# A layer of decayed linear attention and a looked-up gated network: queries and keys made in seven block products for eight, and four operations of the down stage issued earlier

## The reference

```
q = xn Wq;  k_i = xn Wk[i];  v_i = xn Wv[i]        (i = 0, 1, 2; each 512 -> 128)
gate = softmax(xn Wg)                              (3 per row)
blended = sum_i gate_i * ((q k_i^T * w_i) v_i)     (w_i: causal decay, strictly after)
s = blended Wo * out_scale                         (128 -> 512)
h = silu(xn Wgate^T) * (xn Wup^T)                  (512 -> 1376)
out = x + s * silu(h Wdown^T)                      (1376 -> 512)
```

## Time and profile before

| | |
|---|---|
| time, median of 3 runs | 1836.87 us (1836.4 to 1838.73) |
| the profiled execution's own time | 1841.18 us |
| its span in the trace | 1839.1 us |
| PE busy | 97% of the span |
| PE weight loads busy | 77% |
| DVE, POOL, ACT busy | 71%, 56%, 44% |
| mean granted clock of PE | 0.998 |

### The profile page before, as it was taken

How to read it: one execution, slowest core, us unless ns; L and a number is a source line. 1 busy time by engine, 2 the same in 40 slices (tenths; PEclk the granted TensorE clock), 3 DMA queues, 4 the chain that set the end, 5 groups by cost and what they waited for, 6 DMA issues and landing times.

```text
span 1839.1 us, 41728 instructions
## 1 busy us (share of the span) xinstructions
PE 1792.9 (97%) x15944; PEld 1419.5 (77%) x15944; DVE 1302.6 (71%) x2629; ACT 812.7 (44%) x1406; POOL 1026.8 (56%) x1041
## 2 busy tenths in 40 slices
PE   5899999999999999999999999999999999999997
PEld 2337879788787978788787978878796887879786
DVE  6885858686776867677685767768585867758574
ACT  3784444444444443444444444444444444444433
POOL 9303736556473746547374665647375564737363
PEclk9999999999999999999999999999999999999999
DMA  9986685958678676967768696876859686786753
GB/s 219 329 305 175 168 232 162 254 160 228 192 191 219 169 230 165 255 170 196 211 178 221 168 249 163 224 201 173 228 168 237 165 236 181 184 223 168 209 149 112
DMA packets 411028, 370.90 MB, mean 202 GB/s; under 512 B 222577, under 2 KB 278641, under 8 KB 410753
## 3 DMA queue, kind: packets, MB, share of 16 engines
q1 hardware_dynamic: 399824, 361.36, 71.0%
q0 software_dynamic: 11008, 6.89, 2.5%
HBM read 294.34 MB, written 35.52 MB: 179 GB/s over the span
## 4 chain that ended last, share of the span: by engine, by line
PE 90%; DMA 5%; ACT 1%; POOL 1%; issue 1%; DVE 1%; SPq 0%; POOLq 0%; ACTq 0%; DVEq 0%
PE F L1870 44%; PE F L1909 17%; PE B L1750 16%; DMA region<-mixed_half 3%; PE B L1782 2%; PE F L1890 2%; PE B L1757 2%; PE B L1755 2%; PE B L1756 2%; PE F L1657 1%; POOL codes L728 1%; PE F L1755 1%; PE F L1756 1%; PE F L1757 1%; DMA dblocks<-xt 1%
## 5 line engine op out<-in xcount | busy, mean ns | idle before, releaser
L1870 PE MATMUL F<-xtc,ring 128*128 128x256 f16 (+1 forms) x4224 | 497.7, 273 | 0.0
L1870 PEld LDWEIGHTS F<-xtc,ring 128*128 128x128 f16 (+1 forms) x4224 | 416.0, 100 | 42.4
L1909 PE MATMUL F<-ring,region 128*128 128x256 f16 x3360 | 382.5, 273 | 0.0
L1870 PE MATMUL F<-xt,ring 128*128 128x256 f16 (+1 forms) x3168 | 377.2, 273 | 0.0
L1909 PEld LDWEIGHTS F<-ring,region 128*128 128x128 f16 x3360 | 328.0, 98 | 47.9
L1870 PEld LDWEIGHTS F<-xt,ring 128*128 128x128 f16 (+1 forms) x3168 | 310.8, 100 | 33.3
L923 ACT ACTIVATE region<-region 128x512 f16<-128x512 f32 (+3 forms) x256 | 130.3, 509 | 270.8 <-DVE region L1531 115.7
L832 POOL TENSOR_TENSOR region<-hs,region 128x1024 f16<-128x1024 f32 x80 | 175.4, 2192 | 104.1 <-ACT region L923 104.1
L850 POOL TENSOR_TENSOR x_out<-x_out,region 128x512 f32<-128x512 f32 x64 | 81.0, 1266 | 133.7 <-DVE region L1602 133.7
L923 ACT ACTIVATE region<-F 128x512 f32<-128x512 f32 (+2 forms) x168 | 95.9, 573 | 129.6 <-PE F L1909 84.2
L1750 PE MATMUL B<-xt,a_hi 128*128 128x512 f16 x512 | 152.3, 379 | 0.0
(11 more groups left out here) (269 smaller groups left out, 3361.4 us busy)
## 6 DMA issues: line engine op xcount, KB each, us to landing
ring<-blocks SPq DMA_DIRECT2D x546, 256.0 KB, 3.3
ring<-dblocks SPq DMA_DIRECT2D x224, 256.0 KB, 3.5
x_next<-in_x SPq DMA_DIRECT2D x64, 256.0 KB, 4.3
x_out<-in_x SPq DMA_DIRECT2D x64, 256.0 KB, 3.2
out_y<-x_out SPq DMA_DIRECT2D x64, 256.0 KB, 4.9
ring<-blocks SPq DMA_DIRECT2D x112, 128.0 KB, 2.5
ring<-dblocks SPq DMA_DIRECT2D x112, 128.0 KB, 3.1
blocks<-ring SPq DMA_DIRECT2D x35, 256.0 KB, 7.6
```

Of the source, the lines that this page charges most:

```text
L1870: ins = T_.matmul(out_, a, b, start=fresh, stop=False, skip_group_check=True)
L1909: ins = T_.matmul(bank[:, j * HV:(j + 1) * HV], a, b, start=fresh, stop=False, skip_group_check=True)
```

## The change

**Seven products for eight.** Queries and keys become a set of their own, QK = -1, ahead of the six. `queries_keys` now calls the same `product` as the sets. The 512 x 512 matrix [Wq Wk0 Wk1 Wk2], scaled, is the operand in blocks; S1, S2 and S3 are held in the new tensor `qsum`, S4 in place of a block of `a_hi` and `a_lo` that no product uses alone. A product is 2 x 2 x 3 = 12 matmuls of 256 columns, into the banks F0 to F3 in place of B0 and B1. ACT and DVE run `first_copy`, `u2`, `u4`, `c22`, `c12` and `c21` for it, and take the halves of q and the keys from the four result blocks (`qk_high`, `qk_low`) in place of four banks.

**Build.** DVE scales Wq and Wk in place and makes the four sums and their low halves; ACT takes the four high halves, two after step 33 and two after step 34. `plus`, `minus`, the pick matrices, `eye` and `ht` move to other memory.

**Order.** SP issues `blend(3)` after slot 8, ahead of the load of `x_next`, and `turn_sums(1)` after slot 12. ACT issues `x_sums_high(1)` ahead of `partial(2)` in place of after `attn_out(1)`, POOL `x_sums_low(1)` ahead of `finish(0)` in place of after it. Semaphore s_pp counts 49 products a group for 42.

```diff
+    QK = -1
+    SPG = NSET + 1
+    QSUM = {S1: 0, S2: 1, S3: 2}
+    QBASE = {A11: (0, 0), A12: (2, 0), A22: (2, 2 * P), S4: (0, 2 * P)}
...
+        QKB = ((ZC, 2, HALF), (FB[0].rearrange("p (m t) -> p m t", m=2), 0, 0), (YC, 0, HALF), (XC[0], 2, 0))
...
+        QSUM_AT = {NU: (0, 1), NU + 1: (2, 3)}
...
+                    if m == 8:
+                        blend(3)
                     if m == 8 and ahead:
                         sp.wait_ge(s_xh, gi * GT + 2 * GT)
                         sp.sem_inc(s_go, 1)
                         load_x(row_group(i + 1, g))
-                    if m == 10:
-                        blend(3)
-                    if m == 13 and not last:
+                    if m == 12 and not last:
                         turn_sums(1)
...
                     x_sums(1)
+                    x_sums_low(1)
                 finish(0)
-                if not last:
-                    x_sums_low(1)
                 finish(1)
...
+                if b in QSUM_AT:
+                    for n in QSUM_AT[b]:
+                        act.wait_ge(s_scale, 2 + n + 1)
+                        copy(qs_half(n, 0), sums[n]).then_inc(s_ahi, 1)
...
+                def qk_high(n):
+
+                    done = ((s_c22, of_set(gi, QK) + 1), (s_pp, made(gi, QK, 4)), (s_c12, of_set(gi, QK) + 1),
+                            (s_c21, of_set(gi, QK) + 1))[n]
+                    block, j0, t0 = QKB[n]
+                    act.wait_ge(*done)
+                    if n == 0:
+                        act.wait_ge(s_y1, gi * GT + GT)
+                    if j0 == 0:
+                        copy(q32[:, t0:t0 + HALF], block[:, 0], scale=2.0 ** QP).then_inc(s_q32, 1)
+                    copy(qk_hi[:, j0:j0 + 2, t0:t0 + HALF], block, scale=2.0 ** QP).then_inc(s_qk, 1)
+
+                first_copy(QK)
+                if not last:
+                    act.wait_ge(s_dwr[ND - 1], 16)
+                    x_high(0, gi * GT + GT + 1)
+                    x_high(1, gi * GT + GT + 2)
+                for n in range(4):
+                    qk_high(n)
...
                 attn_out(0)
+                if not last:
+                    x_sums_high(1)
                 partial(2)
                 attn_out(1)
-                if not last:
-                    x_sums_high(1)
...
+            def product(i, g, s, p):
+
...
+                if p == 0:
+                    bank, k0, cols = FB[0], 0, lo
+                    pe.wait_ge(*((s_z, gi * GT + FREE) if s == QK else (s_qkl, gi * 4 + 2) if s == 0 else
+                                 (s_sg1, gi * NSET + s)))
+                elif p == 1:
+                    bank, c = FB[1], T2
+                    pe.wait_ge(*((s_g, gi * GT + FREE) if s == QK else (s_u2, prev)))
+                    if s == QK:
+                        pe.wait_ge(s_xtc, 32 * (gi + FREE))
+                        pe.wait_ge(s_alo, len(MATS) + 4)
+                elif p == 2:
+                    bank, c = FB[3], T1
+                    pe.wait_ge(*((s_ca, gi * GT + FREE) if s == QK else (s_c12, prev)))
...
             def queries_keys(i, g):
                 gi = i * GPB + g
-                xh, xl = xt_hi[:, g], xt_lo[:, g]
-
                 for t in range(GT):
                     pe.wait_ge(s_xt[t], 16 * (gi + FREE))
-                for j in range(1 + NH):
...
-                    three(B[j % 2], [(a_hi[:, k, j * D:(j + 1) * D], a_lo[:, k, j * D:(j + 1) * D],
-                                      xh[:, k], xl[:, k]) for k in range(KC)], GRP).then_inc(s_pqk, 1)
+                for p in range(NP):
+                    product(i, g, QK, p)
```

More of the change, by code:

```diff
@@ L234, in attention_ffn_kernel @@
         mixed_half = sb("mixed_half", [P, 2, 2, D], F16)
-        plus = sb("plus", [P, P], F16)
-        minus = sb("minus", [P, P], F16)
+        qsum = sb("qsum", [P, 3, 2, BANK], F16)
         mask = sb("mask", [P, NH, P], F32)
         flip = mixed
+        plus, minus = mixed_half[:, 0, 0], mixed_half[:, 0, 1]
+        pick_hi, pick_lo = (mixed_half[:, 1, n].rearrange("p (q r) -> p q r", q=CG) for n in range(2))
+        eye = hs[:, 3, 0:QR]
+        lutpick = hs[:, 3, QR:QR + CG * CG].rearrange("p (q c) -> p q c", q=CG)
         fade_row = faded[:, :].rearrange("p (h t) -> p h t", h=NH)
@@ L313, in attention_ffn_kernel @@
             pos += n
+        fb = ctx.enter_context(nc.psum_tensor("F", [P, 4, BANK], F32))
+        FB = [fb[:, n] for n in range(4)]
         def halves(k, **dims):
@@ L339, in attention_ffn_kernel, with qs_half @@
         wo32 = q32
+        qs32 = [xp[:, n] for n in range(2)] + [hs[:, 2 * n:2 * n + 2].rearrange("p a t -> p (a t)") for n in range(2)]
+        sums = [v.rearrange("p (k c) -> p k c", k=2) for v in qs32]
+        def qs_half(n, lo):
+            if n < 3:
+                return qsum[:, n, lo].rearrange("p (k c) -> p k c", k=2)
+            return (a_hi, a_lo)[lo][:, 0:2, 2 * P:4 * P]
         staged = region[:, n_oh + KC * QKV:n_oh + KC * QKV + 4 * BANK * 2].bitcast(F16).rearrange(
@@ L516, in attention_ffn_kernel, with shape, of_set, made @@
         FREE = 1
+        def shape(s):
+            return (P, 2) if s == QK else (FM[MS[s][0]], len(MS[s]))
+        def of_set(gi, s):
+            return gi * SPG + s + 1
+        def made(gi, s, p):
+            return of_set(gi, s) * NP + p + 1
         def row_group(i, g):
@@ L1334, in _ @@
                     low_part(LOW_AT[b], MATS.index(LOW_AT[b]))
+            dve.wait_ge(s_ahi, len(MATS))
+            dve.wait_ge(s_alo, len(MATS))
+            for n, cut in ((0, slice(0, CK)), (1, slice(CK, CV))):
+                step(V_.tensor_scalar(a32[:, :, cut], a32[:, :, cut], f_up[:, n:n + 1], None, ALU.mult))
+            b11, b12, b21, b22 = (a32[:, k:k + 2, c:c + 2 * P] for c in (0, 2 * P) for k in (0, 2))
+            for n, (a, b, op) in enumerate(((b21, b22, ALU.add), (sums[0], b11, ALU.subtract),
+                                            (b11, b21, ALU.subtract), (sums[1], b12, ALU.subtract))):
+                if n in (1, 3):
+                    dve.wait_ge(s_scale, 2 + n)
+                V_.tensor_tensor(sums[n], a, b, op).then_inc(s_scale, 1)
+            for n in range(4):
+                dve.wait_ge(s_ahi, len(MATS) + n + 1)
+                V_.tensor_tensor(qs_half(n, 1), sums[n], qs_half(n, 0), ALU.subtract).then_inc(s_alo, 1)
             dve.wait_ge(s_lscale, 3)
@@ new lines, in c22 @@
+                def c22(s):
+                    q, (M, w) = gi * NSET + s, shape(s)
+                    dve.wait_ge(s_u4, of_set(gi, s) + 1)
+                    dve.wait_ge(s_pp, made(gi, s, 3))
+                    if s == QK and gi:
+                        dve.wait_ge(s_yr, gi * GT - GT + 2 + FREE)
+                    if s == ND:
+                        dve.wait_ge(s_hl2, q - 1 + 2 * FREE)
+                    V_.tensor_tensor(ZB[s][0:M, 0:w], pair(2, s), YB[s][0:M, 0:w], ALU.add).then_inc(s_c22, 1)
@@ L1473, in group @@
+                if not last:
+                    dve.wait_ge(s_tt, (gi * 2 + 2) * NTT)
+                    dve.wait_ge(s_xlo, gi * GT + GT)
+                    xhat_tile(gi + 1, 0)
+                u2(QK)
+                u4(QK)
+                if not last:
+                    xhat_tile(gi + 1, 1)
+                c22(QK)
+                qk_low(0)
+                c12(QK)
+                qk_low(1)
+                c21(QK)
+                qk_low(2)
+                qk_low(3)
                 for t in range(GT):
@@ L1762, in scores @@
                 if n == 0:
-                    for done in (s_lg, s_vl, s_vbl):
+                    for done in (s_lg, s_vl, s_vbl, s_qkl):
                         pe.wait_ge(done, gi * GT + GT)
@@ L1874, in group @@
                 for n in range(NPG):
[L1875 removed]
+                    product(i, g, n // NP, n % NP)
                     if n in SCORES:
```

269 lines of the change are left out of this document (120 added, 149 removed).

## The result

| | before | after |
|---|---|---|
| median (lowest to highest) | 1837.01 us (1836.4 to 1838.73), 4 executions | 1812.97 us (1811.18 to 1813.81), 4 executions |
| ratio after/before, 95% interval | | 0.9868 [0.9853, 0.9882] |
| profiled execution, its span | 1841.18 us, 1839.1 us | 1813.45 us, 1811.5 us |

Faster by 24.0 us (the interval of the ratio is 21.7 to 27.0), and by 27.7 us from one profiled execution to the other. The forecast was 1809.0 with a range of 1804 to 1823: the median is 4.0 above the one and inside the other.

The account below looks back on a forecast made before the run. PE was taken as the bound: its own work plus 11.6 us of waits for the blended tile. Terms -19.0 - 11.5 + 1.5 = -29.0 us; 1809 us was taken, range 1804 to 1823.

Parts of the forecast that it names:

- What bounds the kernel: PE's back-to-back work, 104.83 us a group, plus 11.6 us over 15 periods from waits for the last blended tile.
- signs of being wrong: In the trace after: a PE wait ahead of a matmul F<-xtc,qsum, or a period over 104 us.
- Seven products, -19.0: Queries and keys stage: 10.36 us falls to 9.17, saving 1.19 us in each of 16 groups.
- The rival of weight loads that show: Queries and keys stage: loads 15 ns longer than their matmuls save nothing of the 19, giving 1828; chance 0.04.
- blend(3), -11.5: Down stage: the transpose issued ahead of the load lands before PE needs it, so all the wait goes: -11.5 us.
- The moves of the sums, 0: Sums of x reach the group's second product in time, margin 0.8 to 2.5 us: 0, bounds 0 to +1 a border.
- a new wait at the second product: Rival: PE stops at each border for late sums or F1; 1 us a border gives 1824; chance 0.13.
- Banks and silu_out(3), hidden: Second product needs F1, read by silu_out(3) until 0.9 us after the border, against 1.2: hidden while ACT is punctual.
- the edge that I had put at groups like the twelfth: Third and fourth products' banks: late add_c22 delays silu_out(3) in the worst groups, 0 to +0.2 us in a few.
- DVE and ACT in the new set, 0: After product_out(3), DVE's 11 operations take 7.6 us with 10.4 us of room before the values: 0.
- The build, +1.5: End of build: ACT's high halves +1.2 us, DVE's scaling and sums late by +0.3; bounds 0 and +4.
- the first group's chain behind `x_high(0)`: First group: chain waiting for the last write of the down blocks; given only in the build's upper bound of +4 us.

Follow-up runs that it names:

- e1: Kernel before with only blend(3) moved ahead of the x_next load: 1829.1 us against 1835.48 beside it, ratio 0.9965.
- e5: Kernel before with each 512-column matmul of queries and keys made as two of 256: 1839.13 us against 1836.52, ratio 1.0011.
- e3: Kernel after with blend(3) put back after slot 10, behind the load: 1815.62 us, ratio 0.9897 to the kernel before.
- e2: Kernel after with all four moves of order undone, seven products alone: 1814.46 us, ratio 0.9888 to the kernel before.
- e4: Kernel after with x_sums_high(1), x_sums_low(1) and turn_sums(1) back in their old places, blend(3) still in front: 1813.34 us, ratio 0.9879 to the kernel before.
- e6: Kernel after with turn_sums(1) issued after slot 18 in place of 12: 1847.62 us, ratio 1.0068 to the kernel before.
- e7: Kernel after with the first group's x_high(0) and x_high(1) behind its halves of q and keys: 1814.29 us, ratio 0.9881 to the kernel before.
- e8: e7 with the first group's x_sums_high(0) also moved, behind the fourth tile of values: 1812.41 us, ratio 0.9866 to the kernel before.
- e10: Same code as e2, run a second time: 1816.79 us, ratio 0.9889 to the kernel before.
- e9: Kernel before, unchanged, run a second time: 1836.98 us against 1837.51 beside it, ratio 0.9994.

## Why the prediction was right, and where its sizes were off

**What bounds the kernel.** Right: PE's own work plus what it waits for. The bare periods of e1 and of the kernel after show that nothing else is in them. Of the signs of being wrong that the prediction named, one came: a period over 104, the first (105.18), where PE also stood 0.3 us ahead of its first `xtc,qsum`. The other 14 are bare. Those 1.5 us belong to the build's term, below.

**Seven products, -19.0.** Right: 9.17 us, as worked out from 109 ns, and e5 shows that columns set the price. The rival of weight loads that show is thereby out; they are 100 ns and hidden.

**blend(3), -11.5.** The mechanism is right and was shown alone (e1) and undone (e3). The tile was issued at 232.17, as forecast (232.1), and none took over 4.9 us to land. The 2.3 to 6.7 us of the earlier trace rows, median 3.1, were those of all four blended tiles of a group. Taken alone, the 16 `blend(3)` of a trace have a median of 5.6 us before and of 3.0 in e1 and after, while the medians of the other three tiles are 2.3 to 3.1 in all of these. The step that was off is its size, "Ends: nothing comes back, or all 11.6. I take all". In that trace it was 10.6, since 7 x 0.14 = 1.0 of it was the even groups' own work, which I had taken from one odd group. And it was one execution's wait: timed, the move is worth 6.4 with eight products (e1) and less with seven (e2 to e4). I had written that the shorter executions "may have waited less, and then less comes back", and then allowed 1.1 us for it where 5.1 were due by e1. The pair of traces gave back 27.7 because it had an execution that waited long as its base.

**The moves of the sums, 0.** Right in the forecast version: no wait in 15 borders. The margin was stated as 0.8 us at the longest landing and 2.5 at the median; the longest is now 8.7 us, and the sums landed between 2.9 us ahead of the border and 0.8 us after it, where they are needed 1.2 us after it. So the worst border had 0.4 us left. e4 shows that one slot later some borders do wait, e6 what it costs when all do. In the traces of e7 and e8, which have the same order of the sums, they landed as late as 0.9 and 1.3 us after a border, and one period of e8 is 0.05 us long for it. The rival "a new wait at the second product" was thus at its edge, and that the kernel after shows none is in part luck of the execution.

**Banks and silu_out(3), hidden.** Right: it still ends 0.9 us after the border, in every group. The timelines of ACT and DVE there, to the earlier trace rows:

```profile
245.96 0.69 ACT L1187 ACTIVATE region<-F,scale_hf 128x512 f32<-128x512 f32 x1 [1.31 <-PE F L1975]
```

```profile
246.68 0.69 DVE L1677 TENSOR_TENSOR region<-region 128x512 f32<-128x512 f32 x1 [1.30 <-ACT region L1187]
```

245.96 + 0.69 - 245.75 = 0.90. It follows PE and not `add_c22`: `silu_out(2)`, which waits for that, ended 0.6 to 2.2 us ahead of each border, so the edge that I had put at groups like the twelfth didn't show.

**DVE and ACT in the new set, 0.** Right but for the first group. The values on DVE begin 12.03 us into the group, where 12.0 was forecast (their first operation, to the earlier trace rows):

```profile
257.78 0.56 DVE L1593 TENSOR_TENSOR region<-B,fade_v 128x384 f32<-128x384 f32 x1 [0.32 <-ACT logit L950]
```

**The build, +1.5.** Its sum is nearly right and its parts are not. It measured 2.0. The two early pairs of high halves were priced at +1.2, as if ACT had no idle time; ACT took them, partly in time that it had waited before, and the border came 0.46 us later after the last lookup (6.38 to 6.84 us, the same in all traces of either kind). The timeline of ACT and of DVE at the end of the build, to the earlier trace rows:

```profile
136.71 0.60 ACT L950 ACTIVATE ring<-B 128x512 f16<-128x512 f32 x1 [0.48 <-PE B L1766]
137.20 0.65 ACT L950 ACTIVATE xhat_half<-B 128x256 f16<-128x256 f32 x2
137.75 1.14 ACT L950 ACTIVATE qsum<-xp 128x512 f16<-128x512 f32 x2
```

```profile
141.36 0.69 DVE L1394 TENSOR_TENSOR a_lo<-hs,a_hi 128x512 f16<-128x512 f32 x1
```

The last low half ends at 142.05, and PE's second product starts at 142.19 where 140.57 + 1.31 = 141.88 was due: 0.31 late, as forecast (0.3). What I had left in the bounds alone, the first group's chain behind `x_high(0)`, cost 1.24 in that trace and 0.2 to 1.0 in those of e2, e3, e4, e6 and e10. e8 takes it out by moving those copies.

**Summed up.** -19.0 and +2.0 from the traces and -6.4 timed make -23.4, and 24.0 was measured. The agreement is closer than the parts allow. Seven products alone were timed at -21.0 and -20.7 (e2, e10) where these terms give -17.0, and -21.0 with the -6.4 of e1 would make -27.4. So the 5.0 us between the forecast -29.0 and the result are known in kind, a wait sized by one execution that waited long, and how the timed 24.0 splits is known to some 4 us only.

## What to carry to other kernels

A wait that ends on a DMA isn't one number: read it in more than one execution, or undo it by itself and time that, before it goes into a sum. The same holds for a timed median: compare each version with the kernel before that was timed beside it. Count what an engine waits for from the distance of its borders, and take the bare period from a group of each kind, not from one. Where a consumer moves earlier, its producers' place in each in-order queue has to move too, and pushing that place the other way (e6) prices the need; but a move within one engine's queue, as in e7, also delays whoever feeds the next step of that same queue. A wait of TensorE can cost more than its length, as in e6 and e7, where 2.3 and 3.2 us of standing were followed by matmuls at half the clock: look at the granted clock behind each new wait.

## What was not expected of the hardware

The time at which the build ends varies between executions more than the change moves it: the first border lay at 140.16, 140.20, 140.50 and 141.73 us in the four traces with eight products and between 137.29 and 142.19 in the eight with seven, while the way from the last lookup to it was constant, and the change made that way longer by 0.46. That alone spreads the total by several us, and hides effects of about 1 us (e4, e7, e8) in a few timed executions.

The granted clock has a part in it. In 11 of the 12 traces it was at half once or twice between 30 and 83 us. In seven (e1, e5, e9, after, e4, e6, e8) it was so between 74 and 83 us, and there the 54 matmuls from PE's 649th on took 8.5 to 11.1 us; in the other five (before, e2, e3, e7, e10) they took 5.6 to 7.6. The seven have their first borders at 139.5 to 142.2. The four others with seven products have theirs at 137.3 to 138.6, but the kernel before has 140.20. So the clock isn't all of it, and the rest stays open.

The place in SP's queue changes how long a transpose takes to land. Those of `mixed_half`, each the same size, took 2.3 to 4.9 us after, with the load of `x_next` behind `blend(3)`, and up to 6.7 before, with it ahead.
